# A gated cross-attention and mixture-of-experts block: nine step numbers of a hand-written schedule are changed

## What is computed

```python
def block(x, ctx, mask, g_xattn, g_ffn, adj, Wq, bq, Wk, bk, Wv, bv, Wo, bo, gate_w, w1, b1, w2, b2):
    n = layernorm(x)
    Q, K, V = heads(n, Wq, bq), heads(ctx, Wk, bk), heads(ctx, Wv, bv)      # 4 x 16 x 512 x 16
    scores = Q @ K.T / sqrt(16) + adj
    weights = softmax(where(mask == 0, -inf, scores))
    x = x + tanh(g_xattn[0]) * (merge(weights @ V) @ Wo.T + bo)
    n = layernorm(x)
    p = softmax(n @ gate_w.T); e = argmax(p)
    ye = relu(n @ w1[e] + b1[e]) @ w2[e] + b2[e]
    return x + tanh(g_ffn[0]) * ye * p[e]
```

## Time and profile before

| | us |
|---|---|
| median of 3 runs | 567.52 |
| all three runs | 564.27, 567.52, 569.73 |
| time of the profiled execution | 567.52 |
| its span, first to last instruction | 565.6 |
| first DVE tile 12 of batch 0, 1, 2, 3 (L1551) | 43.02, 129.65, 216.89, 301.95 |

### The profile page before, as it was taken

How to read it: one execution, slowest core, us unless ns; L and a number is a source line. 1 busy time by engine, 2 the same in 40 slices (tenths; PEclk the granted TensorE clock), 3 DMA queues, 4 the chain that set the end, 5 groups by cost and what they waited for, 6 DMA issues and landing times.

```text
span 565.6 us, 13534 instructions
## 1 busy us (share of the span) xinstructions
PE 522.7 (92%) x4078; PEld 405.1 (72%) x4127; DVE 299.1 (53%) x908; ACT 303.0 (54%) x675; POOL 303.9 (54%) x461
## 2 busy tenths in 40 slices
PE   7989999989999989999999998779978989999996
PEld 5576666667667657666667665568868989999995
DVE  2776677876577875677866878813610101111111
ACT  4366677656677656778575675544222333333331
POOL 6445476764566674566665546453324454544451
PEclk9999999999999999999999999999998999999999
DMA  8632525302215500115510198788235656555650
GB/s 294 198 110 96 174 92 197 104 20 83 68 63 198 134 20 22 55 35 183 154 43 2 56 296 177 143 299 301 25 117 195 184 184 181 185 191 197 188 189 6
DMA packets 51391, 77.22 MB, mean 137 GB/s; under 512 B 9944, under 2 KB 34600, under 8 KB 51208
## 3 DMA queue, kind: packets, MB, share of 16 engines
q1 hardware_dynamic: 46600, 67.72, 37.5%
q0 software_dynamic: 4096, 8.29, 5.3%
q10 hardware_dynamic: 640, 0.52, 0.3%
HBM read 52.76 MB, written 7.89 MB: 107 GB/s over the span
## 4 chain that ended last, share of the span: by engine, by line
PE 48%; DMA 19%; issue 11%; DVE 9%; POOL 4%; SPq 4%; ACT 4%; another core or an unknown queue 1%; POOLq 1%; DVEq 0%; ACTq 0%
PE bank L941 14%; DMA out_y<-cT,sidx 11%; PE bank L953 8%; PE bank L931 6%; DVE prob L1551 5%; PE bank L834 4%; DMA slot_d<-pair,posi 4%; SPq L345 3%; PE bank L915 2%; PE bank L869 2%; PE bank L1116 2%; PE bank L1031 2%; PE bank L1106 2%; ACT pt L1209 2%; DMA rows<-xn_d,gidx 2%
## 5 line engine op out<-in xcount | busy, mean ns | idle before, releaser
L1551 DVE CUSTOM_DVE_ANT_0 prob<-bank,adjm 128x512 f32<-128x512 f32 x256 | 172.8, 689 | 76.1 <-issue 44.6
L672 POOL TENSOR_SCALAR prob<-prob,negmax 128x512 f32<-128x512 f32 x192 | 133.6, 699 | 124.9 <-DVE negmax L1551 120.0
L1209 ACT ACTIVATE pt<-bank 128x512 f32<-128x512 f32 x256 | 150.1, 594 | 85.3 <-PE bank L941 77.8
L941 PE MATMUL bank<-ident,prob 128*128 128x128 f32 x1024 | 154.9, 274 | 15.1 <-ACT pt L1209 7.6
L941 PEld LDWEIGHTS bank<-ident,prob 128*128 128x128 f32 x1024 | 123.5, 141 | 46.7 <-issue 18.1
L1278 ACT ACTIVATE adjm<-bank,colsm 128x128 f32<-128x128 f32 x184 | 52.3, 368 | 107.9 <-PE bank L1106 84.0
L931 PE MATMUL bank<-w2s 128*128 128x512 bf16 x208 | 79.1, 380 | 3.6 <-DVE negmax L1551 3.3
L1727 DVE TENSOR_TENSOR cT<-bank,maski 128x256 f32<-128x256 f32 x18 | 7.6, 425 | 119.5 <-PE bank L1116 119.5
L1106 PEld LDWEIGHTS bank<-xT,pt 128*128 128x128 f32 x576 | 68.4, 195 | 1.8 <-ACT xT L1272 0.9
L1106 PE MATMUL bank<-xT,pt 128*128 128x128 f32 x576 | 68.7, 278 | 0.7 <-ACT xT L1272 0.7
L953 PE MATMUL bank<-pt,vals 128*32 128x256 f32 x1024 | 68.3, 385 | 0.7 <-DVE vals L1365 0.5
(11 more groups left out here) (192 smaller groups left out, 617.4 us busy)
## 6 DMA issues: line engine op xcount, KB each, us to landing
pt<-in_L_ffn_w SPq DMA_DIRECT2D x19, 1024.0 KB, 10.1
w2s<-parts SPq DMA_DIRECT2D x96, 128.0 KB
w2s<-in_L_ffn_w SPq DMA_DIRECT2D x8, 1024.0 KB, 10.0
maski<-in_mask_Bx1xSxS_ik SPq DMA_DIRECT2D x4, 1024.0 KB, 5.8
w2s<-parts SPq DMA_DIRECT2D x56, 64.0 KB, 2.1
xres<-in_x SPq DMA_DIRECT2D x18, 128.0 KB
x_d<-rows SPq DMA_DIRECT2D x18, 128.0 KB
xn_d<-rows SPq DMA_DIRECT2D x18, 128.0 KB
```

The costliest lines, as they stand in the source:

```text
L672: po.tensor_scalar(prob[:, m], prob[:, m], -1.0, negmax[:, m:m + 1], ALU.mult, ALU.add).then_inc(s_shpool, 1)
L941: mm = pe.transpose(tr_bank[n % NTB][:, c * P:(c + 1) * P], prob[:, n % TILES % NB, c * P:(c + 1) * P], ident[:])
L1209: act.activation(pt[:, g % 2, :, j, q2 * P:(q2 + 1) * P], tr_bank[c % NTB][:].rearrange("p (c q) -> p c q", c=QT), ACT.Exp).then_inc(s_cac ...
L1551: ve.tensor_tensor_reduce(out=prob[:, m % NB], in0=sc_bank[m % NS][:], in1=adjm[:, qt], scale=-1.0, scalar=BIG, op0=ALU.add, op1=ALU.min, ...
```

## The change

Nine numbers of the tables are changed; no operation is added or removed.

- "gate" of rows 0 and 1: PE's step 44 becomes 43. "gate" of row 3: 68 becomes 66. Their readers on DVE move along.
- "next q 0": step 20 becomes 21; with it its second half on PE (21 to 22), `parts` on ACT (22 to 23), `rest` on DVE (23 to 24), and the two splits on POOL (24 and 25 to 25 and 26).
- the four scatters: steps 54, 59, 62, 67 become 53, 55, 57, 59; the wait for them 73 becomes 72. In the last batch the third one goes from 46 to 45.
- the layer norm of batch b+2: POOL's part from step 67 to 66, DVE's four scalings from 69, 70, 72, 73 to 67, 69, 71, 73.

```diff
     TAIL_A = [(15, "heads", 0), (18, "heads", 1), (23, "turn", 0), (25, "turn", 1), (29, "out", 0),
-              (33, "out", 1), (38, "normed", 0), (41, "normed", 1), (44, "gate", (0, 1)), (51, "rank", 0)]
+              (33, "out", 1), (38, "normed", 0), (41, "normed", 1), (43, "gate", (0, 1)), (51, "rank", 0)]
     USES = sorted([(10, "values", 0), (11, "values", 1)] + TAIL_A
                   + [(12, "next x", 0), (14, "next x", 1), (17, "next ctx", 0), (19, "next ctx", 1),
-                     (20, "next q", 0), (26, "next k", 0), (30, "next q", 1), (35, "next k", 1)]
+                     (21, "next q", 0), (26, "next k", 0), (30, "next q", 1), (35, "next k", 1)]
                   + [(45, "heads", 2), (46, "heads", 3), (50, "turn", 2), (52, "turn", 3), (53, "out", 2),
                      (56, "out", 3), (61, "normed", 2), (63, "gate", (2,)), (64, "normed", 3),
-                     (68, "gate", (3,))], key=lambda use: use[0])
+                     (66, "gate", (3,))], key=lambda use: use[0])
...
-    STATS_STEPS, RSTD_STEP, NORM_STEPS = (61, 62, 64, 65), 67, (69, 70, 72, 73)
+    STATS_STEPS, RSTD_STEP, NORM_STEPS = (61, 62, 64, 65), 66, (67, 69, 71, 73)
...
-    SLOT_STEPS, SCATTERED_STEP = ((54, 59, 62, 67), (41, 43, 46, 47)), (73, 60)
+    SLOT_STEPS, SCATTERED_STEP = ((53, 55, 57, 59), (41, 43, 45, 47)), (72, 60)
```

## The result

The changed kernel took 574.12 us (median of 4 runs, 572.71 to 574.99), the kernel before 567.9 us (median of 4 runs, 564.27 to 569.73). The ratio is 1.0112, with a 95% interval of 1.007 to 1.0153: 1.1% slower, where 0.9% was forecast. The profiled execution took 572.78 us, 5.26 us more than the one before. (The diff changes thirteen numbers of the tables, not the nine of which the title speaks.)

What follows compares the result with a forecast made beforehand. PE was taken as the bound, busy 522.7 of 565.6 us. Terms 2.1 + 1.5 + 1.3 + 0.3 = 5.2 us on 567.52 gave 572.7 us, 0.9% slower; own range 570 to 575.5, whole range 565.5 to 577.

Steps and rivals of the forecast that it cites:

- Next q: Step 20 to 21: DVE's `rest` falls behind tile 24, so PE's "turn 1" waits 0.7 us in batches 0 to 2; 2.1 us.
- Gate of rows 0 and 1: Step 44 to 43: PE reaches the gate before ACT has written `x2T` and waits 0.5 us in three batches; 1.5 us.
- Scatters: Second scatter now ahead of tile 56 on POOL, so PE waits at tile 57; 0.2 + 0.1 + 1.0 = 1.3 us.
- The hold of L1417: Third scatter meeting DVE's row scaling on the shared ports: at fullest 3 x 0.44 = 1.3 us more; taken as nothing.
- Layer norm and gate of row 3: Batch boundaries: scaling ahead of tile 68 adds 0.1 in batch 0, the gate 0.1 in batches 0 and 2; 0.3 us.
- The relief wins: Rival: PE's gaps at both boundaries shrink, new bank and gate waits aren't felt; 565.3 us, chance 0.12.
- All of it is absorbed: Rival: PE's earlier losses are waited for anyway in DVE-bound steps 48 to 53; about 568.5 us, chance 0.10.
- POOL's crowd is carried in all batches: Rival: scatters cost 3 x 1.0 us, the scaling ahead of tile 68 1.2 us twice; +9.0, 576.5 us, chance 0.25.
- Time outside the attention: Code after the attention: time should be the same; a difference there would be none of the terms.

Runs made afterwards that it cites:

- the scatters alone: Kernel before with only the four scatters moved to steps 53, 55, 57, 59 and their wait to 72; 567.15 us, ratio 0.9972.
- the second scatter alone: Kernel before with only the second scatter moved from step 59 to 55; 568.47 us in one execution.
- the two kernels with equal code: Equal up to step 66 in batch 0: kernel before with only the four scatters and their wait moved, 567.15 us; change with steps 20 and 44 restored, 570.43 us.
- the layer norm alone: Kernel before with only POOL's layer norm part at step 66 and DVE's scalings at 67, 69, 71, 73, fourth scatter still at 67; 571.55 us in one execution.
- the gate alone: Kernel before with only the gate of row 3 moved from step 68 to 66; 570.69 us in one execution.
- the change without two parts: The change with next q 0 back at step 20 and the gate of rows 0 and 1 back at step 44; 570.43 us, ratio 1.0043.

## Why the prediction was right, and where it was not

The forecast was 572.7 us, and 574.12 was measured (572.78 in the profiled execution); sum of the terms 5.2 us, measured 5.65 in the attention.

- **Next q**, forecast 3 x 0.7: right, 3 x 0.67, alone and in the change. The wait is where it was put, and nothing later gives it back.
- **Gate of rows 0 and 1**, forecast 3 x 0.5: right, 3 x 0.47, alone and in the change.
- **Scatters**, forecast 0.2 + 0.1 + 1.0 = 1.3: measured 0.73 + 0.58 + 0.57 = 1.88, within the bounds of 0.4 to 3.0, and differently made. POOL's crowd, which is all that the term held, is 0.17 + 0.05 + 0.58 = 0.80 (batch 0 from the scatters alone, the others from the second scatter alone). It is as forecast in batches 0 and 1, and 0.4 too high in batch 2. There the transposes of tile 57 do come 1.0 us late, counted from step 56 (287.43, where the schedule of before, moved by the later start and the delays up to there, has 281.30 + 0.40 + 4.76 = 286.46). But "nothing late enough behind it to hide it" failed. In the kernel before, PE waits 0.49 us for ACT at the next transposes, which is the row below; in the changed kernel it comes to them late enough (289.51) and doesn't wait, so about 0.4 us are hidden. The other 1.1 us of the 1.88 are the hold of L1417, for which the sum had no term.

```profile
283.76 0.63 PE L941 MATMUL bank<-ident,prob 128*128 128x128 f32 x4 [0.49 <-ACT pt L1209]
```

- **The hold of L1417.** The prediction took nothing for VectorE and GpSimd meeting on their ports, and priced its fullest effect as 3 x 0.44 us, the length of one L1417. Its sentence that failed is "DVE's tiles 62 and 63 are not moved by it". The crowd moved the third scatter onto L1417, which waited for the scatter, for 0.57 to 0.58 us in each batch, with DVE's tiles behind it. PE lost 0.57 us by it in batch 0, as the two kernels with equal code show, nothing in batch 2, and up to 0.53 us in batch 1, where no kernel has all of this crowd without the hold. That nothing was the one term put down without a reason from the rows, although the 0.59 us of L1417 beside POOL's L612 stood in the trace of before. In the Trainium skill, on the page "SBUF — State Buffer", section "SBUF: two separate sides", the lock works in both directions: whoever starts first has the pair and the other "fully blocks". I had priced only the direction in which VectorE holds GpSimd's DMA. The rows agree with the other one where L1417 ends 0.12 us after the scatter. They disagree with "for the whole instruction", as far as the records of the profile give an instruction's length: L1417 also ran inside a scatter in its normal 0.41 us. It started 0.21 us into it (the scatters alone, batch 0), 0.48 us into it (only the second early, batch 2), and 0.35 us into it (batch 1 of the kernel before and of seven kernels that leave it as it is there).
- **Layer norm and gate of row 3**, forecast 0.3: measured 0.50 / -0.47 / 0.33, 0.36 in all. That the sum fits is luck. Batch 0 was forecast as 0.2 and batch 2 as 0.1, and both cost more; the -0.47 after batch 1 is at the place where kernels that touch nothing near it lie between -0.95 and +0.26. The mechanism in batch 0 is the one described: the power, at 121.48, is 0.39 (the later start of tile 12) + 1.88 (the delays up to there) behind the old schedule, which puts it at 119.21 where it was at 120.37, 1.2 us earlier; and the scaling ahead of tile 68 spends that. The boundary moved by -0.73 us with the scatters alone, by +0.72 with the layer norm alone and by 0.00 with the gate alone. These sum to -0.01, and the change has +0.50, because the relief is counted twice: in each of the first two kernels alone the power comes 1.16 us earlier, and it can do so only once. Where the power is as early and the scalings stay in their place, the boundary is 0.73 to 0.78 us shorter; with the scalings moved it is 0.50 to 0.72 us longer. So moving them costs 1.2 to 1.5 us in batch 0. The layer norm alone has the fourth scatter between the power and the subtraction of tile 68, and the change hasn't, which fits the 0.22 us between these two; that step was not tried by itself. In batch 2 the two parts add up: 0.18 from the gate, as in the gate alone, and 0.15 that the scatters alone have too, for which the forecast had nothing ("tiles 58 and 60, whose transposes come late enough").
- **The rivals.** "The relief wins" needed next q and the gate to cost nothing; they cost 3.4 us (forecast 3.6), and the relief that it counted on, 0.73 to 0.78 us in batch 0, was found only in kernels that leave the scaling where it was. "All of it is absorbed" is out, since the delay stays at its level from each of these steps to the end of the batch. "POOL's crowd is carried in all batches" came nearer in the pattern, with 0.73, 0.58 and 0.57 us, but not in the cause: the crowd alone is 0.17, 0.05 and 0.58, and the hold brings two of the three up to it.
- **Time outside the attention**: forecast none, measured +0.4 and -0.9 us in untouched code, less than the same kernel differs by from itself there.
- **How near the total came.** 5.2 against 5.65 us is in part luck: next q and the gate are right one by one, but a missing 1.1 us (the hold) and terms that were too small by 0.5 us (boundaries of batches 0 and 2) met others that were too large by 0.4 us (batch 2), 0.2 us (next q and the gate) and the unreadable -0.47. In the chances, 0.4 of 0.53 and most of 0.25 make about 0.45 for "over 1% slower", not 0.40; 1.1% was measured, just past that line.

## What to carry to other kernels

When a step is moved in a schedule of in-order engines, look up the last reader that frees its buffer and put that reader's new neighbour beside the user that waits: two such pairs gave 3.4 of 5.65 us here, where 3.6 were forecast. A wait that a removed instruction leaves open is only won if the waiter keeps its place; move it forward as well, and it stands in front of work it used to overlap. After moving a GpSimd instruction, look for an SBUF-to-SBUF instruction of VectorE that now starts inside it, and then ask whether anything waits for that one: the same hold cost 0.57 us in one batch and nothing in another. Look at single durations, since a mean over a group (442 ns for most 0.41 and some 0.59 us) hides such meetings. Before adding up parts that were measured alone, ask whether two of them win the same wait.

## What the runs showed of the hardware

- A VectorE tensor_scalar on float32 from SBUF to SBUF (L1417, 128x256, 0.41 us) that starts 0.22 us into an indirect DMA of GpSimd (1.08 us) takes 0.98 to 0.99 us and ends 0.12 us after it; it did so in 3 of 3 batches of the change, 3 of 3 of the change without two parts, and 2 of 3 with the scatters alone. Started 0.53 us into it: 0.68 us, end again 0.12 us after. Started 0.56 to 0.57 us into it: 0.61 us, end 0.09 us after (batch 2 of the same three kernels). Started 0.66 us into it: 0.46 us, end 0.10 us after (the gate alone, batch 0). Started 1.0 us into it: 0.41 us. But started at 0.21 and at 0.48 us it was not held in one case each, nor at 0.35 us in 8 of 8 (batch 1 of the kernel before and seven others). So the start alone does not decide, and what does isn't shown.
- It isn't the DMA alone. The same instruction takes 0.59 to 0.61 us in batches 0 to 2 of all 14 traces where it starts 0.71 to 0.72 us into POOL's L612 (1.16 us), and 0.82 us where it starts 0.01 us into a subtraction L672 (0.69 us; the scatters alone, batch 0). It ends 0.15 us after either.
- Two executions of the same program agree in every tile's start to 0.04 us within the attention, except where ACT stands for something that is no engine: 2.74 us in one trace, 0.34 and 1.33 in another. It stands for 1.78 us at another boundary in another kernel. The cause stays open. It makes single boundaries differ by up to 1.2 us, more than most of what was moved here.
